# A pre-norm transformer layer on one core: 128-row tiles in the down projection, and key and query projections one stage earlier

## The reference

```python
def attn(x):                                    # x after layer norm
    q, k, v = x @ Wq + bq, x @ Wk + bk, x @ Wv + bv      # 16 heads of 16
    scores = q @ k.T / sqrt(16) + slope[head] * distance[key]
    scores = where(causal, scores, lowest)
    return softmax(scores) @ v @ Wo + bo

def quantize(w):
    return clip(round(w / (mean(abs(w)) + 1e-8)), -1, 1)

def ffn(x):                                     # x after layer norm
    x1, x2 = x @ quantize(w1).T, x @ quantize(w2).T      # 256 -> 704
    return (sigmoid(x1) * x2) @ quantize(w3).T           # 704 -> 256

x = x + attn(layernorm(x))
x = x + ffn(layernorm(x))
```

## Time and profile before

| | us |
|---|---|
| median of 3 runs (651.88 to 655.70) | 655.19 |
| the profiled execution | 657.24 |
| its span, first to last instruction | 655.5 |
| head, up to the first score matmul | 39.1 |
| chunk 0, steps 0 to 15 | 39.1 to 112.3 |
| chunk 1, steps 16 to 47 | 112.3 to 247.6 |
| chunk 2, steps 48 to 95 | 247.6 to 428.9 |
| chunk 3, steps 96 to 159 | 428.9 to 617.5 |
| tail | 617.5 to 655.5 |
| PE, DVE, ACT, POOL busy | 608.8, 462.1, 358.3, 184.7 |

### The profile page before, as it was taken

One profiled execution on the slowest core, in us unless ns is written; L12 is line 12 of the kernel. 1 busy time (PEld: TensorE's weight loads), 2 busy tenths in 40 slices (PEclk: granted clock), 3 DMA queues, 4 the chain that ended last, 5 costly groups with the idle time before them and its releaser, 6 DMA issues.

```text
span 655.5 us, 10867 instructions
## 1 busy us (share of the span) xinstructions
PE 608.8 (93%) x3484; PEld 374.6 (57%) x3484; DVE 462.1 (70%) x1194; ACT 358.3 (55%) x766; POOL 184.7 (28%) x394
## 2 busy tenths in 40 slices
PE   7878787999899989899999999999999999999897
PEld 5545445656566655465556675655555556555486
DVE  5756887667777866478887788788888888411175
ACT  3335535646553636456655555467576664667521
POOL 7445522252423231322112332103200400423300
PEclk9969888999999989899999999999999999999999
DMA  6985643545321205434131131146141310011001
GB/s 192 266 228 149 164 115 94 148 141 140 79 65 44 65 26 149 145 100 113 37 84 34 35 98 33 50 121 162 34 115 34 78 41 1 2 43 42 1 17 33
DMA packets 27277, 57.65 MB, mean 88 GB/s; under 512 B 5396, under 2 KB 15124, under 8 KB 23636
## 3 DMA queue, kind: packets, MB, share of 16 engines
q1 hardware_dynamic: 27220, 56.95, 31.9%
HBM read 41.87 MB, written 14.80 MB: 86 GB/s over the span
## 4 chain that ended last, share of the span: by engine, by line
PE 73%; DVE 14%; issue 5%; ACT 4%; DMA 3%; POOL 1%; SPq 1%; ACTq 0%; POOLq 0%
PE pO L1024 19%; PE pS L1011 18%; PE pM L991 16%; PE pM L966 5%; DVE pm L1185 4%; PE pM L975 3%; DVE pM L1188 3%; PE pM L908 2%; PE pM L952 2%; ACT probs L839 2%; PE pM L916 2%; PE pS L975 1%; DMA work<-in_L_attn_x 1%; PE pS L908 1%; PE pS L966 1%
## 5 line engine op out<-in xcount | busy, mean ns | idle before, releaser
L839 ACT ACTIVATE probs<-pS 128x512 f32<-128x512 f32 (+3 forms) x640 | 300.4, 546 | 194.7 <-PE pS L1011 192.1
L1185 DVE TENSOR_REDUCE pm<-pM 128x1 f32<-128x512 f32 x384 | 239.3, 681 | 50.5 <-PE pM L991 50.0
L1011 PE MATMUL pS<-qst,kst 128*128 128x512 f32 (+3 forms) x640 | 248.1, 408 | 9.4 <-DMA qst<-mT 4.4
L991 PE MATMUL pM<-kst,qst 126*128 126x512 f32 (+3 forms) x640 | 230.1, 388 | 14.6 <-DVE pm L1188 5.8
L1011 PEld LDWEIGHTS pS<-qst,kst 128*128 128x128 f32 x640 | 119.7, 191 | 99.2 <-issue 49.6
L991 PEld LDWEIGHTS pM<-kst,qst 126*128 126x128 f32 x640 | 122.1, 194 | 56.8 <-DVE pm L1188 14.5
L1188 DVE CUSTOM_DVE_ANT_0 pM<-pM,mask 128x128 f32<-128x128 f32 (+3 forms) x256 | 118.5, 520 | 41.6 <-PE pM L991 41.2
L724 POOL TENSOR_SCALAR_AFFINE_SELECT probs<-probs 128x128 f32<-128x128 f32 x256 | 77.8, 315 | 243.5 <-ACT probs L839 235.6
L1024 PE MATMUL pO<-probs,vals 128*17 128x512 f32 (+3 forms) x1280 | 136.4, 540 | 0.0
L1024 PEld LDWEIGHTS pO<-probs,vals 128*17 128x17 f32 x1280 | 30.1, 97 | 68.0 <-issue 41.2
L1153 DVE SCALAR_TENSOR_TENSOR work<-work,pM 128x256 f32<-128x256 f32 (+1 forms) x38 | 15.9, 419 | 31.5 <-ACT work L829 27.8
(11 more groups left out here) (146 smaller groups left out, 407.6 us busy)
## 6 DMA issues: line engine op xcount, KB each, us to landing
kst<-parts SPq DMA_DIRECT2D x80, 256.0 KB
parts<-qk_hl SPq DMA_DIRECT2D x32, 256.0 KB, 3.2
qst<-parts SPq DMA_DIRECT2D x32, 256.0 KB, 4.1
ctx_dram<-ctx_raw SPq DMA_DIRECT2D x15, 256.0 KB, 3.9
xin<-in_L_attn_x SPq DMA_DIRECT2D x5, 512.0 KB, 4.6
out<-work SPq DMA_DIRECT2D x8, 256.0 KB, 2.2
work<-ctx_dram SPq DMA_DIRECT2D x7, 256.0 KB
work<-rden_dram SPq DMA_DIRECT2D x7, 256.0 KB
```

The costliest lines, as they stand in the source:

```text
L839: nc.scalar.activation(probs[:, n % PSLOTS, q0:CH], pS[:, n % SBANKS, q0:CH], ACT.Exp)\
L991: pe.matmul(max_bank(x)[:, 0:N], qst[0:R_MAX, u % QSLOTS, h, t * P:(t + 1) * P], kst[0:R_MAX, n % KSLOTS, h, 0:N], start=True, stop=True). ...
L1011: pe.matmul(pS[:, n % SBANKS, q0:CH], kst[0:R_END, sl, h, b:b + P], qst[0:R_END, u % QSLOTS, h, q0:CH], start=True, stop=True).then_inc(sc ...
L1185: nc.vector.tensor_reduce(dst, bank, AX.X, ALU.max).then_inc(max_free, 1)
```

## The change

- The last tile of w3 and of the hidden values is filled up with zeros to 128 rows, and the down matmuls use all rows (GpSimd clears two blocks in the head, VectorE one in the tail).
- `head_between` holds all four k and q groups of chunk 1, at turns 3, 7, 11 and 15 of unit 0.
- Chunk 0's side groups: v of chunk 1 in steps 0 and 1, gamma in step 3, then the transposes and k and q of chunk 2 in steps 4 to 9. Chunk 1 keeps chunk 2's v, in its first two steps. Chunk 2's x is loaded in the head and normalised at steps 1 to 3.
- The negated maxima are split before the transpose: one transpose of 32 columns, one copy, one transfer.
- The first unit of chunk 1 also has early turns. `add_bo` of chunks 0 and 1 moves from the third to the seventh step of the next chunk.

```diff
         if c == 0:
-            lst = lst[4:6] + [("gamma",)] + lst[6:] + [None] * 5
+            lst = lst[6:] + [None, ("gamma",)] + pre_groups(2)[:6]
+        if c == 1:
+            lst = lst[6:]
...
-    LN_AT = {0: 12, 1: 27, 2: -9, 3: -9}
+    LN_AT = {0: 1, 1: 27, 2: -9, 3: -9}
...
-    head_between = {G - 1: ("k", 1, 0), 2 * G - 1: ("q", 1, 0)}
+    head_between = {(i + 1) * G - 1: g for i, g in enumerate(pre_groups(1)[2:6])}
...
             def load_m(v):
                 sp.wait_ge(mT_ok, v + 1)
-                for part in range(2):
-                    sp.dma_start(qst[R_MAX + part:R_MAX + part + 1, v % QSLOTS, :, :].bitcast(F32)
-                                 .rearrange("o h (t n) -> o (h t) n", n=P),
-                                 mT[:, part, :]).then_inc(m_in, 16)
+                sp.dma_start(qst[R_MAX:R_MAX + 2, v % QSLOTS, :, :].bitcast(F32).rearrange("a h (t n) -> a (h t) n", n=P),
+                             mT[:, :]).then_inc(m_in, 16)
...
             load_m(0)
+            store_parts(("k", 1, KT - 1))
+            store_parts(("q", 1, KT - 1))
+            load_x(2)
             load_raw(1, w2)
...
-                if ph == 3 and c + 2 < NCH:
+                if ph == 3 and 1 <= c < NCH - 2:
                     load_x(c + 2)
...
+            link(nc.gpsimd.memset(w3T[FROWS[FT - 1]:P, FT - 1, :].bitcast(F32), 0.0))
+            link(nc.gpsimd.memset(hT[FROWS[FT - 1]:P, :, FT - 1, :].bitcast(F32), 0.0))
...
-            split_lo(("k", 1, 0))
-            split_lo(("q", 1, 0))
+            for g in head_between.values():
+                split_lo(g)
...
-                if ph == 2 and c >= 1:
+                if c >= 1 and ph == (6 if c < NCH - 1 else 2):
                     add_bo(c - 1)
...
-                if s < 2:
-                    size_of_weights(1 + s)
+                if s in (1, 2):
+                    size_of_weights(s)
...
-                                ins = pe.matmul(w[:, i * D:(i + 1) * D], hT_of(g)[0:r, part, f, i * P:(i + 1) * P],
-                                                w3T[0:r, f, :], start=f == 0 and part == 0,
+                                ins = pe.matmul(w[:, i * D:(i + 1) * D], hT_of(g)[:, part, f, i * P:(i + 1) * P],
+                                                w3T[:, f, :], start=f == 0 and part == 0,
...
-                early = EARLY_TURNS if j == 0 and units[u][0] == 0 else 0
+                early = EARLY_TURNS if j == 0 and u <= NHG else 0
...
+                if m == FT - 1 and g[1:3] == (NCH - 1, 1):
+                    nc.vector.memset(hT_of(g)[rows:P, :, m, :].bitcast(F32), 0.0)
...
-                nc.vector.tensor_reduce(nm[:, :], pm[:, u % 2, :, 0:units[u][0] + 1], AX.X, ALU.max, negate=True)\
-                    .then_inc(nm_ok, 1)
+                link(nc.vector.tensor_reduce(nm[:, :], pm[:, u % 2, :, 0:units[u][0] + 1], AX.X, ALU.max, negate=True))
+                link(nc.vector.tensor_scalar(nm_hl[:, 0, :].bitcast(F32R), nm[:, :], SHIFT, None, ALU.add))
+                nc.vector.scalar_tensor_tensor(out=nm_hl[:, 1, :].bitcast(F32R), in0=nm[:, :], scalar=SHIFT,
+                                               in1=nm_hl[:, 0, :], op0=ALU.add, op1=ALU.subtract).then_inc(nm_ok, 1)
...
-                link(nc.vector.tensor_scalar(mT[:, 0, :].bitcast(F32R), m, SHIFT, None, ALU.add))
-                nc.vector.scalar_tensor_tensor(out=mT[:, 1, :].bitcast(F32R), in0=m, scalar=SHIFT, in1=mT[:, 0, :],
-                                               op0=ALU.add, op1=ALU.subtract).then_inc(mT_ok, 1)
+                nc.vector.tensor_copy(mT[:, :], max_bank(x)[0:2 * G * TPC, 0:P]).then_inc(mT_ok, 1)
```

More of the change, by code:

```diff
@@ L287, in preln_layer @@
         nm = sb("nm", [P, G * TPC])
+        nm_hl = sb("nm_hl", [P, 2, G * TPC])
         dens = sb("dens", [P, H * CH // P])
-        mT = sb("mT", [G * TPC, 2, P])
+        mT = sb("mT", [2 * G * TPC, P])
         pS = es.enter_context(nc.psum_tensor("pS", [P, SBANKS, CH], F32))
@@ L970, in side_group @@
                     for i in range(2):
-                        for f, r in enumerate(FROWS):
+                        for f in range(FT):
                             if i == 0:
@@ L998, in swap_max @@
                 pe.wait_ge(nm_ok, u + 1)
-                pe.transpose(max_bank(x)[0:G * TPC, 0:P], nm[:, :], ident[:, :]).then_inc(max_ready, 1)
+                pe.transpose(max_bank(x)[0:2 * G * TPC, 0:P], nm_hl[:, :, :].rearrange("p a k -> p (a k)"), ident[:, :])\
+                    .then_inc(max_ready, 1)
             def scores(s, h):
@@ L1006, in scores @@
                 if j == 0 and h == 0:
-                    pe.wait_ge(m_in, 32 * (u + 1))
+                    pe.wait_ge(m_in, 16 * (u + 1))
                 q0 = diag(u, j)
@@ L1203, in split_max @@
                 if u >= 1:
-                    dve.wait_ge(m_in, 32 * u)
-                m = max_bank(x)[0:G * TPC, 0:P]
-                link(nc.vector.tensor_scalar(mT[:, 0, :].bitcast(F32R), m, SHIFT, None, ALU.add))
-                nc.vector.scalar_tensor_tensor(out=mT[:, 1, :].bitcast(F32R), in0=m, scalar=SHIFT, in1=mT[:, 0, :],
-                                               op0=ALU.add, op1=ALU.subtract).then_inc(mT_ok, 1)
+                    dve.wait_ge(m_in, 16 * u)
+                nc.vector.tensor_copy(mT[:, :], max_bank(x)[0:2 * G * TPC, 0:P]).then_inc(mT_ok, 1)
             def invert(c):
```

## The result

In 20 runs the changed kernel took 657.1 us (median; 654.5 to 664.5) beside 654.4 for the kernel before on the same chip: ratio 1.005, 95% interval 1.0035 to 1.0066. (The ratios of this document leave out runs more than 1.5% above the fastest of their kernel and are not quotients of the two medians: here the ratio is worth 3.3 us, the medians differ by 2.7.) I had forecast 648.3 with a range of 639 to 657. The profiled execution took 656.98, its span is 655.3.

The account below looks back on a forecast made before the run. The prediction took TensorE as the bound, nearly always busy from chunk 1 on, with idle room in head and chunk 0. Terms +0.9 +1.3 +8.3 -3.8 -7.8 -5.3 -0.5 gave -6.9 us: 648.3 us, range 639 to 657.

Parts of the forecast that it names:

- Padding, -5.3: Down projections: full 128-row matmuls save 4.0 us between scores and 1.8 in the tail, less 0.5 for clearing.
- Chunk 1, -7.8: Chunk 1: its ten dense steps lose projections, transposes and turns (-9.9 us), against 0.8 for VectorE and 1.3 of wait.
- the denominators' chain: Chunk 1, before the output projection: a 13.4 us chain from step 22 does not shorten; 1.3 us of wait (0 to 3).
- Head, +0.9: Before the first score: added k and q projections delay it from 39.1 to 40.0 us (0 to +2.5).
- Steps 0 to 3, +1.3: Start of chunk 0: step 4 begins at 62.5 us against 60.3, +1.3 beyond the head.
- The wait in step 2: Chunk 0: TensorE stands still about 6 us (2 to 11) until q of unit 2 lands behind added stores and x.
- Steps 4 to 15, +4.0: Rest of chunk 0: +8.3 us in steps 4 to 9, -3.8 in steps 10 to 15, -0.5 for the third unit's maxima.
- a stall of 4.5 in step 9: Chunk 0: ScalarE's q write waits for a late store behind loads, stopping TensorE 4.5 us (2 to 8).
- chunk 0's third unit: Chunk 0: TensorE's 0.5 us wait for this unit's maxima goes, -0.5 us.
- The later swaps, 0: Later transposes of the maxima: they lose only a DMA that nobody waits for, so no time changes.
- The sum against one execution: Whole run: the summed difference of -6.9 us, read from one profiled execution, was applied to the median of 655.19.
- the one in which SyncE's queue becomes the bound: Rival: transfers in steps 2 and 9 land at their late ends, with one more half-clock stretch: 657.8 us, chance 0.12.

Follow-up runs that it names:

- pad_only: Kernel before with the padding alone (last tile of w3 and hidden values zeroed to 128 rows, down matmuls on all rows): 649.9 us, ratio 0.9905.
- a_b3l_bo2r: Changed kernel with three qk_hl buffers, k and q loaded ahead of x and w3, bias addition at step 18, denominators' reciprocals at step 19: ratio 0.9915.
- a_noswap: Changed kernel with the maxima split after the transpose again, as in the kernel before: ratio 1.0012 to the kernel before.
- a_store: Changed kernel with the q and k loads of step 7 moved behind the store of that step's q: ratio 1.0033 to the kernel before.
- pad_rden: Kernel before with the padding and the denominators' reciprocals and their way through memory at step 19 instead of 21: ratio 1.0039.
- a_b3l_bo2: Changed kernel with three qk_hl buffers, k and q loaded ahead of x and w3, and the bias addition back at step 18: ratio 0.9985.
- move_only: Kernel before with only the projections and transposes moved; padding, bias addition and maxima as they were: 662.2 us, ratio 1.0096.

## Why the prediction was wrong

- **Padding, -5.3: right** (-6.2, with an interval of 4.6 to 7.9; pad_only), and with it the reading of two rows against the Trainium skill's rule. By place it was 0.8 between scores and 0.6 in the tail; a group saves about 0.75 in either, since the slower starts reach into the matmul behind it.
- **Chunk 1, -7.8 (-9.4 with padding): right in sum, wrong inside.** The ten steps closed up by more than I said, partly because 3.4 us of half clock are gone there, and steps 24 to 26 gave 4.3 us back where I had 1.3 for the denominators' chain. I had named the chain and its length; a_b3l_bo2r shows it. I had let its transfers be quicker with less traffic beside them: GpSimd got the rows 9.3 us after the reciprocals' store was issued (149.15 to 158.49), 8.0 before (142.48 to 150.50).
- **Head, +0.9: wrong in size**, +3.4 in the trace. I had the wait and its time, but took the q projection as covered by turn 15's reduction. It ran at half clock, 2.94 us, and held the transpose from 37.65 to 38.79.
- **Steps 0 to 3, +1.3: wrong in size**, +2.8. The wait in step 2 is there (4.7 us for 6), but with it came 6.8 us of half clock where I had allowed for a start at half clock.
- **Steps 4 to 15, +4.0: this part failed**, with +8.0. I had 24.5 us for steps 4 to 9, a stall of 4.5 in step 9, and then 27.5 for steps 10 to 15. The stall came in step 10, so the terms have to be compared without it: steps 4 to 9 took 26.2, the stall 6.27, steps 10 to 15 without it 27.5, and the half microsecond that I had taken off for chunk 0's third unit did not come. So the path that I had for the last six steps was right. Mis-sized were the stall, by 1.8, and steps 4 to 9, by 1.7. Of the latter, 0.9 is my own adding up: 17.2 + 6.9 + 0.8 + 1.0 - 1.9 is 23.9 us of TensorE, not about 23 (the trace has 23.55). What makes the rest is not shown; 6.8 us of half clock from 67.5 in place of 3.4, and a wait of 1.5 us for VectorE's normalised x at the start of step 4, lie there.
- **The later swaps, 0: wrong.** I looked at the DMA that went and not at two operations that came into the path from the last turn to the transposition: 4.2 us at nine swaps in the trace, 2.5 by a_noswap.
- **The sum against one execution.** I carried the profiled execution's sum over to the median. That execution lies 2.9 us above the median of 20 runs; it contained up to 4.5 us at step 53, of which most others lack 3 or more.

The misses add up. The forecast was -6.9 and the medians differ by +2.7, which is 9.6 apart: head 2.5, steps 0 to 3 1.5, steps 4 to 15 4.0, chunk 1 0.2, chunks 2 and 3 -2.0 (step 53 and the padding gave more than the swaps took), tail 0.5, and 2.9 for the execution that the rows came from.

Of the rivals, the one in which SyncE's queue becomes the bound gave 657.8, which is the time that came. The match in time is luck. It was right in kind: both stalls are transfers that land late. In size the two waits are 11.0 us, near the forecast's 10.5, not the 17 that it asked for; the rest of the time came from the terms above. The chance of 0.12 was too low because I had gathered the losses of several small mechanisms under one large one.

The basic error is the sentence that moved work is free as far as it falls into idle time. The idle time of chunk 0 was waiting on two buffers and one queue, and the projections that moved in need just these. Idle time is room only for work that does not use what the engine is waiting for.

## What to carry to other kernels

Before work is moved into a stage with idle time, list for each piece the buffers, stores and loads that go with it, and follow them through the issuing queue: one store behind 5.6 us of loads cost more than three projections. A third buffer removed that wait, another place in the queue only passed it on (a_store). When a stretch is made denser, look for the chain whose length does not shrink with it and issue that one earlier, but not ahead of a store that someone waits for (pad_rden). And take one trace of the kernel before as one execution: a wait of several us in it may not be in the median.

## What the runs showed of the hardware

- Four matmuls of 64 rows among 24 cost 0.56 us against 128 rows (3.44 and 2.88 us), 0.75 with the matmul behind them, and 32 of them 6 us in a whole run. The matmuls of 128 rows right behind them start as far apart as they do (0.21 to 0.22 us in place of 0.12). Zeroed rows were cheaper than fewer rows in this stream.
- Two q loads issued beside 0.5 MB of x and the weights landed after 8.5 and 9.6 us (7.3 and 7.8 before); a store of 0.25 MB behind loads after 6.8 and 8.1, and the same one ahead of them (a_store) after 2.8 and 3.0.
- Waits of 4 us or more on TensorE (57.7 and 99.5 in after, 144.2 in pad_rden, 153.7 in a_b3l_bo2) each came with 6.8 us at 1.2 GHz. So did every other wait of that length in these traces but one (7.1 us in step 10 of move_only, with 10.2). Stretches as long came without such a wait too: from 67.5 in after the longest wait is 1.5 us. Where one follows a stall, the stall costs more than its length: the projection behind the last of them took 3.75 us, and 1.99 at full clock.
